# Key feature map from one exponential on ScalarE and one VectorE instruction, in place of three activations and a GpSimd addition

## What is computed

```python
def _feature_map(t):
    return jax.nn.elu(t) + 1.0
Q = (x @ Wq.T + bq).reshape(b, s, H, D)
K = (x @ Wk.T + bk).reshape(b, s, H, D)
V = (x @ Wv.T + bv).reshape(b, s, H, D)
Q = _feature_map(Q)
K = _feature_map(K)
KV = jnp.einsum('bshd,bshe->bhde', K, V)
K_sum = K.sum(axis=1)
Z = 1.0 / (jnp.einsum('bshd,bhd->bsh', Q, K_sum) + 1e-06)
out = jnp.einsum('bshd,bhde,bsh->bshe', Q, KV, Z)
```

## Time and profile before

| | |
|---|---|
| median of three executions | 570.28 us (568.74 to 573.35) |
| profiled execution, span of the core | 532.9 us |
| around the span (median less span) | 37.4 us |
| TensorE busy | 478.5 us, 90% |
| DVE busy | 394.3 us, 74% |
| GpSimd busy | 348.1 us, 65% |
| ScalarE busy | 335.1 us, 63% |

### The profile page before, as it was taken

One profiled execution on the slowest core, in us unless ns is written; L12 is line 12 of the kernel. 1 busy time (PEld: TensorE's weight loads), 2 busy tenths in 40 slices (PEclk: granted clock), 3 DMA queues, 4 the chain that ended last, 5 costly groups with the idle time before them and its releaser, 6 DMA issues. The chain is left out here.

```text
span 532.9 us, 13968 instructions
## 1 busy us (share of the span) xinstructions
PE 478.5 (90%) x3686; PEld 445.1 (84%) x3687; DVE 394.3 (74%) x1324; ACT 335.1 (63%) x805; POOL 348.1 (65%) x727
## 2 busy tenths in 40 slices
PE   4999899999999999999999999999954499999991
PEld 4988789999898999989999988888843498989990
DVE  4666478888887888788878877877854288888881
ACT  4334467667666757766676776766632488888870
POOL 0463234677777677777777778887776067877774
PEclk9999899999999999999999999999995599999996
DMA  8951000111121112711111211110013567852220
GB/s 298 281 168 34 14 23 14 39 35 33 34 56 33 30 37 81 238 30 51 39 30 36 55 31 31 42 35 22 18 38 99 155 196 220 241 160 82 78 79 31
DMA packets 31578, 43.24 MB, mean 81 GB/s; under 512 B 8541, under 2 KB 23840, under 8 KB 31539
## 3 DMA queue, kind: packets, MB, share of 16 engines
q1 hardware_dynamic: 21650, 27.12, 17.4%
q0 software_dynamic: 9216, 15.12, 8.9%
q10 hardware_dynamic: 672, 0.53, 0.3%
HBM read 26.45 MB, written 17.17 MB: 82 GB/s over the span
## 5 line engine op out<-in xcount | busy, mean ns | idle before, releaser
L521 POOL DMA_INDIRECT sorted_rows<-rows,place x64 | 75.1, 1174 | 39.7 <-POOL place L516 28.7
L608 POOL DMA_INDIRECT out<-result,result_id x64 | 62.6, 978 | 30.2 <-DVE result L1059 13.7
L684 ACT ACTIVATE k_neg<-k_in 114x512 f32<-114x512 f32 x32 | 20.3, 634 | 59.7 <-DVE k_in L961 59.7
L1078 PE MATMUL b_kvp<-wkv_hi,xnT_hi 128*114 128x512 f32 x128 | 52.9, 413 | 0.0
L696 ACT ACTIVATE xn<-rows_all,shift,rstd 114x256 f32<-114x256 f32 (+1 forms) x64 | 34.9, 593 | 27.6 <-issue 24.2
L498 POOL TENSOR_TENSOR rstd<-ve,half_neg 114x2 f32<-114x2 f32 x64 | 47.0, 734 | 5.3
L1079 PE MATMUL b_kvp<-wkv_lo,xnT_hi 128*114 128x512 f32 x128 | 50.4, 394 | 0.0
L1080 PE MATMUL b_kvp<-wkv_hi,xnT_lo 128*114 128x512 f32 x128 | 50.2, 392 | 0.0
L495 POOL TENSOR_SCALAR ve<-mv 114x2 f32<-114x2 f32 x64 | 15.3, 239 | 53.2 <-DVE mv L840 29.3
L550 POOL TENSOR_TENSOR k_sb<-k_exp,k_relu 114x512 f32<-114x512 f32 x32 | 41.2, 1287 | 5.8 <-issue 4.4
L1078 PE MATMUL b_kvp<-wgu_hi,xsT_hi 128*128 x128 | 37.7, 294 | 6.3 <-DVE xsT_lo L778 6.3
(11 more groups left out here) (174 smaller groups left out, 1771.3 us busy)
## 6 DMA issues: line engine op xcount, KB each, us to landing
rows_all<-sorted_rows SPq DMA_DIRECT2D x64, 130.0 KB
rows_all<-in_x SPq DMA_DIRECT2D x16, 432.0 KB, 4.8
rows_all<-in_txt SPq DMA_DIRECT2D x32, 154.0 KB
rows_all<-in_wgu SPq DMA_DIRECT2D x8, 256.0 KB, 4.5
sorted_rows<-rows,place POOLq DMA_INDIRECT x64, 3.7
rows_all<-in_wdown SPq DMA_DIRECT2D x8, 128.0 KB, 4.7
out<-result,result_id POOLq DMA_INDIRECT x64
rows_all<-in_w_tok SPq DMA_DIRECT2D x2, 384.0 KB, 4.1
```

Of the source, the lines that this page charges most:

```text
L521: G.indirect_dma_start(out=scratch[0:EXPERTS * REGION, :], out_offset=bass.IndirectOffsetOnAxis(ap=place[:, k, b:b + 1], axis=0), in_=rows ...
L608: G.indirect_dma_start(out=out, out_offset=bass.IndirectOffsetOnAxis(ap=result_id[:, k:k + 1], axis=0), in_=result[:, k, :], in_offset=Non ...
L1078: T.matmul(to, left_hi, right_hi, start=start, stop=False)
```

## The change

The key's feature map becomes max(min(exp(k), 1), k + 1). For negative k the exponential lies above k + 1 and below 1; for positive k it is cut to 1 and k + 1 is larger. The bias bk is raised by 1 once, before the loop, so that k_in holds k + 1. ScalarE makes exp(k_in - 1) in one activation. DVE then makes k_sb in one instruction from k_exp and k_in, behind v_sb and ahead of the residual. GpSimd's addition goes.

```diff
+        one_neg = sb("one_neg", [P, 1])
...
-            k_neg = sb("k_neg", [TOK, 2, D], at=room)
-            k_relu = sb("k_relu", [TOK, 2, D], at=room)
...
-                if i.within(PAIRS):
-                    p = i
-                    until, until2 = ahead(pool, p.upto()), ahead(pool, p.upto(1))
-                    pool.wait_ge(s_prep, 1)
-                    pool.wait_ge(kv_parts, until)
-                    if p.had(1):
-                        pool.wait_ge(kvm_done, until2)
-                    G.tensor_tensor(k_sb[:], k_exp[:], k_relu[:], ALU.add).then_inc(k_ready, 1)
...
                     act.wait_ge(k_in_ready, p.upto())
                     if p.had(1):
                         act.wait_ge(k_ready, p.upto(1))
-                    S.activation(k_neg[:], k_in[:], ACT.Relu, scale=-1.0).then_inc(k_neg_ready, 1)
-                    S.activation(k_relu[:], k_in[:], ACT.Relu).then_inc(k_in_used, 1)
-                    act.wait_ge(k_neg_ready, p.upto())
-                    S.activation(k_exp[:], k_neg[:], ACT.Exp, scale=-1.0).then_inc(kv_parts, 1)
+                    S.activation(k_exp[:], k_in[:], ACT.Exp, bias=one_neg[0:TOK, :]).then_inc(kv_parts, 1)
...
+            V.memset(one_neg[:], -1.0)
...
                     dve.wait_ge(kvp_done, p.upto())
                     if p.had(1):
-                        dve.wait_ge(k_in_used, p.upto(1))
+                        dve.wait_ge(k_ready, p.upto(1))
+                    else:
+                        dve.wait_ge(bk_ready, 1)
                     V.tensor_tensor(k_in[:], b_kvp[0:TOK, :, 0:D],
                                     bkv_s[:, 0:D].rearrange("p (b d) -> p b d", b=1).to_broadcast([TOK, 2, D]),
                                     ALU.add).then_inc(k_in_ready, 1)
...
                     last.then_inc(v_ready, 1)
+                    dve.wait_ge(kv_parts, p.upto())
+                    V.scalar_tensor_tensor(k_sb[:], k_exp[:], 1.0, k_in[:], ALU.min, ALU.max).then_inc(k_ready, 1)
...
                 dve.wait_ge(s_bias_dma, 48)
+                V.tensor_scalar(bkv_s[:, 0:D], bkv_s[:, 0:D], 1.0, None, ALU.add).then_inc(bk_ready, 1)
```

More of the change, by code:

```diff
@@ L291, in build @@
         k_in_ready = sem("k_in_ready")
-        k_in_used = sem("k_in_used")
         gu_hi_ready = sem("gu_hi_ready")
         gu_lo_ready = sem("gu_lo_ready")
-        k_neg_ready = sem("k_neg_ready")
         k_ready = sem("k_ready")
         v_ready = sem("v_ready")
+        bk_ready = sem("bk_ready")
         room_ready = sem("room_ready")
```

## The result

| | before | after |
|---|---|---|
| first comparison, median (4 runs each) | 569.62 us | 577.43 us (574.39 to 580.88) |
| ratio after to before | | 1.0161, 95% interval 1.0082 to 1.024 |
| second comparison, on another chip (10 and 6 runs) | 536.4 us | 543.11 us (542.25 to 545.69) |
| ratio | | 1.0114, 95% interval 1.0098 to 1.013 |

The change makes the kernel slower by 1.1 to 1.6%. 576.2 us was predicted. The first comparison alone is wide: 1.0161 x 569.62 is 9.2 us more (4.7 to 13.7). The second is the tighter one: 1.0114 x 536.4 is 6.1 us more (5.3 to 7.0; the medians themselves differ by 6.7), and 5.9 was predicted.

A forecast was written before the change was run, and what follows sets the result against it. The bound was taken to be a circle from router product through DVE's qT, GpSimd's chain and xn2T to the next. Start -4.3, loop +7.6, later pairs +1.75, end +0.8 gave +5.9 on 570.3: 576.2 us; range 572 to 581.

The forecast's parts named there:

- The circle through GpSimd's chain: Loop: router's product, qT, GpSimd's chain, xn, xn2T, next router product set the pace; 0.1 us longer stalls TensorE up to 0.1.
- The hold by two SBUF operands: Loop: DVE's new instruction, reading two SBUF operands, holds a GpSimd instruction starting beside it, 0.48 us a turn on the mean.
- The loop: Pairs 6 to 24: each turn 0.40 us longer, 19 x 0.40 = 7.6 us lost; bounds 0 and 0.63 a turn.
- 0.09 for mv2: Loop: den starts later on DVE, so the statistics mv2 come up to 0.18 us later, worth 0.09 us a turn.
- -0.17 for what comes back: Loop: a later router product lets GpSimd's earlier run meet qT later, so qT's hold shrinks by 0.17 us a turn.
- Pairs 24 to 29: Pairs 25 to 29: wgu_lo holds the new instruction, which then holds so_far by 0.44; 0.35 us a turn, 1.75 us.
- The end: Pairs 30, 31 and last run: wgu_lo delays the new instruction and residual, 0.8 us lost; bounds 0.2 and 1.2.
- The start: Pairs 0 to 2: shorter waits for k_sb and a held clock, less a later residual, gain 4.3 us; bounds 2.6 and 4.7.
- The clock's 1.6 us: Start: with 0.5 us of TensorE idle instead of 2, the clock stays at 2.4 GHz, gaining 1.6 us.
- The third rival: Loop: new instruction 0.3 us late, so the Q product waits for the residual besides the holds; +10.4, 580.7 us; chance 0.12.
- The first rival: Loop: the new instruction isn't caught beside GpSimd's, only the start's gain and 0.5 for mv2 stay; 566.5 us; chance 0.14.
- the second: Pairs 25 to 29: GpSimd's load is the bound, 1.29 us less a pair frees it, no hold; 562.0 us; chance 0.06.

The follow-up runs named there:

- e_nobias: The changed kernel with the exponential's bias operand taken away, so it makes exp(k + 1); 575.21 us, ratio to before 1.0126.
- e_psum: The changed kernel with DVE's new instruction reading K without its bias from PSUM in place of k_in; 567.69 us, ratio to before 0.9959.
- e_mix: The changed kernel's key map for pairs 0 to 2 only, the old map from pair 3 on; 532.27 us where before takes 536.24, ratio 0.993.
- d_half: The kernel before plus one DVE instruction behind v_sb, both operands from SBUF, 256 elements, result unread; ratio to before 1.0063.

## Why the prediction was right

**The bound and the mechanism** held. The circle through GpSimd's chain sets the pace before and after; in turns 5 to 29 the router's load starts 0.04 to 0.06 us behind xn2T's end. The hold by two SBUF operands is all but 0.2 to 0.6 us of what turns 6 to 31 lose, shown by one operand moved to PSUM and by an added instruction of either kind.

**The loop.** 19 x 0.40 = 7.6 us was said, 5.9 measured, 0.31 a turn. The step that was off is "I take 0.63 for the exp": it takes 0.73, for its bias operand, and the new instruction comes 1.45 to 1.48 us behind k_in instead of 1.36 to 1.40. That is just late enough for L493 to slip through in three of four turns, so that L494 is caught for 0.3 in place of L493 for 0.48. e_nobias restores the earlier start and the catch, and loses 6.9 us in these turns, 0.36 each: so 1.0 of the 1.7 us is this step.

The trace takes the terms further apart. What the new instruction adds to the instructions that it catches sums to 6.7 us in these 19 turns, 0.35 a turn, where 0.48 was said: 2.4 us too much. The other two terms, 0.09 for mv2 and -0.17 for what comes back, made -1.5 us together. With the operand in PSUM, where the new instruction holds nothing, the loop takes 198.30 us, before 198.23 to 198.47: together they make nothing. The 0.17 had its sign wrong in the mechanism: the hold by qT, mostly on the last instruction of rstd, doesn't shrink, it grows from 4.1 to 6.2 us in the 19 turns, and it costs nothing, since the GpSimd instruction behind it starts 0.64 to 0.68 us behind qT's start in both kernels (in before in 17 of 19 turns). These terms sum to 6.7 us; where the last 0.8 of the measured 5.9 stays I could not find.

**Pairs 24 to 29**: 1.75 said, 1.8 measured, by half of the mechanism. so_far is held as said (0.67 to 0.69 us for 0.22), but the new instruction, said to be held by wgu_lo in all of them, is so only in pair 25 (1.30 us); in pairs 26 to 29 it keeps its 0.69 to 0.70. **The end**: 0.8 said, 1.8 and 2.9 measured. In pair 31 wgu_lo holds the new instruction longer than I took from pair 30's row, and so_far is held behind it:

```profile
387.18 1.83 DVE L962 SCALAR_TENSOR_TENSOR k_sb<-k_exp,k_in 114x512 f32<-114x512 f32 x1
```

```profile
387.16 1.28 POOL L552 TENSOR_TENSOR wgu_lo<-rows_all,wgu_hi 128x512 fp32r<-128x512 f32 x1
388.40 0.67 POOL L530 TENSOR_TENSOR so_far<-so_far,chosen 114x16 bf16<-114x16 bf16 x1
```

Why the two profiles of after differ there by 1.1 us I did not follow up.

**The start.** -4.3 us was said; the marks give -2.9 against executions of before whose clock fell and -1.3 against those whose clock held. Turns 4 and 5 then lose 0.4, which no term of the sum had, as it counted the hold from pair 6 on; e_psum, without the hold, loses 0.1 there. The first two scores products, after:

```profile
59.66 1.19 PE L1128 MATMUL b_att<-v_sb,k_sb 114*128 114x136 f32 x8 [0.40 <-DVE k_sb L962]
67.68 1.17 PE L1128 MATMUL b_att<-v_sb,k_sb 114*128 114x136 f32 x8 [0.84 <-DVE attn L884]
```

The first wait shrinks by 1.6 us (1.7 was said). The second was to go whole (1.4); DVE's attn was late next, with 0.84, and 0.3 is what was gained of 1.10. The step failed because I asked what releases the product and not what comes after that. The clock's 1.6 us has the right size but isn't always there. Stretches of 2 us with the granted clock third from the end, before on chip C:

```profile
60.00:62.00 2.00, 0.81 (x5) 0.81 (x6) 0.00 (x0) 2.00 (x7) 1.38 (x2) 0.93 0.01 4
62.00:64.00 2.00, 2.00 (x10) 1.89 (x10) 1.36 (x2) 0.83 (x3) 0.00 (x0) 0.50 0.00 0
```

and after:

```profile
60.00:62.00 2.00, 2.00 (x16) 1.79 (x15) 0.74 (x2) 2.00 (x6) 0.00 (x0) 1.00 0.00 0
62.00:64.00 2.00, 2.00 (x11) 1.53 (x10) 1.90 (x6) 0.12 (x1) 0.00 (x0) 1.00 0.02 4
```

Of six profiles in which TensorE idles the 2.0 us there, the clock fell from 2.4 to 1.2 GHz in three; of seven with 0.3 to 0.4 us of idle, in none. 32.04 less 30.43 is the 1.6.

**The rivals.** The third rival's sign, the Q product right behind the residual, is there in every turn from 2 on (its first load starts 0.05 to 0.10 us behind the residual's end; 0.31 to 0.56 from turn 3 on in before and in e_mix, where nothing stands ahead of the residual). It costs nothing that can be seen: e_psum has the same 0.05 to 0.11 and a loop of 198.30. The first rival was wrong, and the second too.

**How much of it was luck.** The single errors are large beside the sum: 1.7 us too much in the loop, 1 to 2 too little at the end, 0.4 missing in turns 4 and 5, and 1.4 to 3 too much gain at the start. They cancel only in part: by the marks after is 7.0 to 9.5 us above before (333.7 and 334.8 against 325.4 to 326.6). The two profiled executions of after took 1.2 and 2.6 us more than the median of theirs, which is part of the way from there to the 6.1 us of the ratio. So the mechanism was right, and that 5.9 falls on 6.1 is luck.

## What to carry to other kernels

An instruction that moves from GpSimd to an idle DVE isn't free for GpSimd: where both its inputs lie in SBUF, whatever small GpSimd instruction starts beside it ends only some 0.78 us behind its start (512 elements; 0.3 to 0.5 us lost for one of 0.23), and a dependent chain of such small instructions was caught, in more or fewer turns, at each of the three places tried. Leave one input in PSUM where the values allow it (here they don't, the bias would be missing), or keep the instruction away from the chain; here the new form is worth having only where its latency is waited for, at the start. And when a wait is taken away, look up the second-latest arrival before counting the whole of it as gain.

## What I had not expected of the hardware

The hold works both ways, and long: beside wgu_lo (1.28 us) DVE's instruction of 0.69 us took 1.83, and one of 0.42 took 3.2 in d_half, where GpSimd's k_sb followed. The same program takes 536 us on two chips and 570 on a third; the difference lies in the third part, and in the 19 turns from mark 5 to 24 they agree to 0.3 us. A [P, 1] bias operand costs an activation 94 ns.
